# Four-layer convolution network on one core: the routing's first linear layer has its weights loaded during the attention, into columns of the last four blocks of x; those blocks are sent later, and unread products fill PE's gaps

## The reference

```python
p = x.reshape(b, c, 16, h // 16, 16, w // 16).mean(axis=(3, 5))
r = relu(einsum('bcij,oc->boij', p, conv_w) + conv_b)      # 16 channels x 256 positions
r = relu(r.reshape(b, -1) @ fc_w.T + fc_b)                 # 4096 -> 256, "first linear layer" below
rw = sigmoid(r.reshape(b, 4, c))
cw = einsum('beo,eoikl->boikl', rw, w_experts)             # 3x3 kernels of a convolution in 16 groups
out = grouped_conv(x, cw)
```

## Time and profile before

| | |
|---|---|
| median of 3 runs | 2512.54 us (2510.32 to 2512.96) |
| profiled execution | 2514.1 us, span 2512.3 us, mean granted clock 0.936 |
| PE | busy 2145.5 us (85%), 7223 records |
| DVE | 1876.6 us (75%) |
| ACT | 1435.7 us (57%) |
| POOL | 1426.0 us (57%) |
| chain that ended last | PE 48%, issue 12%, ACT 11%, DVE 10%, POOL 10%, DMA 6% |
| DMA | 172.76 MB, mean 69 GB/s |

### The profile page before, as it was taken

The page is one execution under the profiler, slowest core; times in us unless marked ns, Lnnn a source line. Parts: engine busy times, 40 slices in busy tenths (PEclk is TensorE's granted clock), DMA queues, the critical chain, the costliest instruction groups (busy, mean ns, idle before and its releaser), DMA issues.

```text
span 2512.3 us, 28673 instructions
## 1 busy us (share of the span) xinstructions
PE 2145.5 (85%) x7223; PEld 1124.5 (45%) x7223; DVE 1876.6 (75%) x3247; ACT 1435.7 (57%) x2268; POOL 1426.0 (57%) x1287
## 2 busy tenths in 40 slices
PE   2898869897968999997988977698989599999798
PEld 2397535443543333333335964353345333333343
DVE  6556766599957999985865668566999489999755
ACT  1843544386865767663346446236778467777532
POOL 2332009498947888872322400485989388888532
PEclk9988989999989999997997998799999799999899
DMA  5000283500001112224720006533000011212344
GB/s 184 1 1 1 87 296 94 190 1 1 1 1 26 40 41 56 42 51 142 238 44 1 1 1 222 191 101 152 1 1 1 11 26 38 59 38 48 88 118 118
DMA packets 199337, 172.76 MB, mean 69 GB/s; under 512 B 72535, under 2 KB 175327, under 8 KB 195831
## 3 DMA queue, kind: packets, MB, share of 16 engines
q1 hardware_dynamic: 199159, 170.78, 23.5%
HBM read 81.69 MB, written 72.29 MB: 61 GB/s over the span
## 4 chain that ended last, share of the span: by engine, by line
PE 48%; issue 12%; ACT 11%; DVE 10%; POOL 10%; DMA 6%; SPq 1%; DVEq 0%; ACTq 0%; POOLq 0%
PE PSUM L2264 8%; PE PSUM L731 6%; PE PSUM L2085 5%; DMA BIG<-BIG 4%; PE PSUM L1053 3%; POOL BIG L932 3%; PE PSUM L2128 3%; PE PSUM L2142 2%; PE PSUM L2284 2%; DVE PSUM L1117 2%; PE PSUM L1045 2%; POOL BIG L1765 2%; POOL BIG L1762 2%; PE PSUM L2100 2%; PE PSUM L2133 1%
## 5 line engine op out<-in xcount | busy, mean ns | idle before, releaser
L848 DVE TENSOR_TENSOR BIG<-PSUM,BIG 128x512 f32<-128x512 f32 x576 | 390.7, 684 | 92.4 <-PE PSUM L1045 48.0
L932 POOL TENSOR_TENSOR BIG<-BIG 128x512 f32<-128x512 f32 x320 | 407.0, 1272 | 63.6 <-ACT BIG L1019 28.6
L1117 DVE SCALAR_TENSOR_TENSOR PSUM<-BIG,VECS,PSUM 128x1024 f32<-128x1024 f32 x224 | 288.2, 1287 | 38.3 <-PE PSUM L2085 33.2
L772 POOL TENSOR_TENSOR BIG<-TOEP,BIG 128x384 f32<-128x384 f32 x84 | 98.2, 1195 | 317.6 <-DVEq L1542 317.6
L1045 PE MATMUL PSUM<-BIG,SELB 120*128 120x512 bf16 x576 | 211.7, 386 | 64.6 <-DMA BIG<-BIG 58.3
L1053 PE MATMUL PSUM<-BIG,CSTS 128*128 128x512 f32 x512 | 266.2, 601 | 0.0
L2085 PE MATMUL PSUM<-BIG,WDW 128*128 128x512 f32 x512 | 234.3, 602 | 12.4 <-ACT BIG L1989 12.4
L2264 PE MATMUL PSUM<-BIG 128*128 128x381 f32 (+1 forms) x576 | 189.1, 492 | 12.9 <-DVE BIG L779 12.9
L1045 PEld LDWEIGHTS PSUM<-BIG,SELB 120*128 120x128 bf16 x576 | 50.8, 97 | 305.4 <-DVE BIG L848 149.3
L2085 PEld LDWEIGHTS PSUM<-BIG,WDW 128*128 128x128 f32 x512 | 97.5, 193 | 140.3 <-issue 115.7
L1762 POOL TENSOR_TENSOR BIG<-BIG 128x1024 f32<-128x1024 f32 x64 | 151.1, 2360 | 10.3 <-POOL BIG L1765 10.3
(11 more groups left out here) (360 smaller groups left out, 5159.9 us busy)
## 6 DMA issues: line engine op xcount, KB each, us to landing
spill<-X SPq DMA_DIRECT2D x18, 1024.0 KB, 6.4
back_spill<-BIG SPq DMA_DIRECT2D x32, 576.0 KB, 3.4
X<-x SPq DMA_DIRECT2D x32, 512.0 KB, 7.4
rows_spill<-X SPq DMA_DIRECT2D x64, 256.0 KB, 4.2
out<-BIG SPq DMA_DIRECT2D x64, 256.0 KB, 3.6
BIG<-rows_spill SPq DMA_DIRECT2D x28, 512.0 KB, 5.2
X<-back_spill SPq DMA_DIRECT2D x14, 896.0 KB, 11.5
BIG<-fc SPq DMA_DIRECT2D x8, 1024.0 KB, 9.7
```

The lines of the kernel that those rows point to most:

```text
L772: eng.tensor_tensor(to.rearrange("p (x c r) -> p x c r", x=3, r=WROW), TOEP[:, y].unsqueeze(1).unsqueeze(1).broadcast_to([P, 3, WCH, WROW] ...
L848: dve.tensor_tensor(img(product_buffer(b, q)), img(PSUM[:, (k + q) % 2, :]), pch(c, XBASE, dy, dx), ALU.mult).then_inc(df_p, 1)
L932: pool.tensor_tensor(a, a, x, ALU.add).then_inc(df_add, 1)
L1117: return dve.scalar_tensor_tensor(out=rows8(to), in0=strip(c, base, dy, dx), scalar=vc(weights, j), in1=rows8(acc), op0=ALU.mult, op1=ALU.add)
```

## The change

The weights' tile FCT moves from WTAIL into WN: for unit o of WN, columns 640 to 1151, which are the blocks 5 to 8 (`FC_FROM` = 9 - 2*256/128 = 5). RB stays where it was. The sync queue issues the four `fc` transfers ahead of the window loop, after a wait for the first `mha_pe` of the pair. In the window loop all nine spills stay where they were in order, but only blocks 0 to 4 are read back there. Behind the loop come the wait for all squares, RT, then a wait for the second `rt_pe` (the end of L2233), then blocks 5 to 8. PE gets products of 128x512 with the constant matrix "mean" into PSUM bank 2, which nobody reads: four after the attention's output stage, one after the group norm, three after L2233, four after L2239.

```diff
+WARM = (4, 1, 3, 4)
...
+FC_FROM = WINDOWS - 2 * FC // W
...
-        FCT = r.take(RED, 2, FC)
+        FCT = WN[:, :, FC_FROM * W:WINDOWS * W].rearrange("p u (h f) -> p u h f", h=2)
+        r.at += RED * 2 * FC
...
                 def spread(w):
 
-                    sp.wait_ge(moved[w % 2], pair * MOVES[w % 2] + (w // 2 + 1) * 16)
+                    sp.wait_ge(moved[w % 2], pair * MOVES[w % 2] + (SPREAD[w % 2] if w >= FC_FROM else (w // 2 + 1) * 16))
...
+                sp.wait_ge(mha_pe, pair * 3 + 1)
+                settle(sp)
+                for j in range(4):
+                    sp.dma_start(FCT[:, 4 * j:4 * j + 4], fc[:, 4 * j:4 * j + 4]).then_inc(fc_in[j // 2], 16)
                 for w in range(WINDOWS):
                     sp.wait_ge(o_x, pair * NS + (window_strip(w) + 1 + CREDIT))
-                    if w == WINDOWS - 1:
-                        sp.wait_ge(l1_sq, (pair + 1) * (2 * NS) + CREDIT)
-                        for j in range(4):
-                            sp.dma_start(FCT[:, 4 * j:4 * j + 4], fc[:, 4 * j:4 * j + 4]).then_inc(fc_in[j // 2], 16)
-                        sp.dma_start(RT, rt_spill).then_inc(rt_in, 16)
                     sp.dma_start(spill[w], X[:, STEP * w:STEP * w + WROW, :].rearrange("p r x -> p (r x)")).then_inc(moved[w % 2], 16)
-                    if w >= 1:
+                    if 1 <= w <= FC_FROM:
                         spread(w - 1)
-                spread(WINDOWS - 1)
+                sp.wait_ge(l1_sq, (pair + 1) * (2 * NS) + CREDIT)
+                settle(sp)
+                sp.dma_start(RT, rt_spill).then_inc(rt_in, 16)
+                sp.wait_ge(rt_pe, pair * 3 + 2)
+                settle(sp)
+                for w in range(FC_FROM, WINDOWS):
+                    spread(w)
...
+                def warm(n):
+
+                    for _ in range(n):
+                        pe.matmul(PSUM[:, 2, :], cs("mean"), CSTS[:, 0:CH], start=True, stop=True)
+
                 in_turn(pe, NS // 2, 0, 1, step)
 
+                warm(WARM[0])
                 group_norm(pair * 4 + 1)
+                warm(WARM[1])
                 pe.wait_ge(l1_mom, pair * 16 + 5)
...
                 ins.then_inc(rt_pe, 1)
+                warm(WARM[2])
                 pe.wait_ge(rt_dve, pair * 16 + 16)
...
                 ins.then_inc(rt_pe, 1)
+                warm(WARM[3])
```

## The result

| | before | after |
|---|---|---|
| median of 5 runs each | 2512.54 us (2510.32 to 2515.6) | 2522.57 us (2519.57 to 2526.82) |
| ratio to before, 95% interval | | 1.0041 (1.0026 to 1.0056) |
| profiled execution | 2514.1 us, span 2512.3 | 2519.57 us, span 2517.8 |
| PE records | 7223 | 7271 (the fillers' 24 per pair) |

The forecast was 2512.9 us with 2507 to 2520 around it. The kernel became 10.0 us slower, clear of the 5.0 us that count as a difference.

What follows compares the result with a forecast made beforehand. The grouped convolution's start was taken to bound the kernel, with ACT's late blocks setting it after the change. Pair 0 at +0.9 and pair 1 at -0.5 us summed to +0.4: 2512.9 us from 2512.54, range 2507 to 2520.

Steps and rivals of the forecast that it cites:

- What bounds the kernel: Routing of each pair: the grouped convolution's start moves the end by as much; ACT's input is close behind as second limit.
- Part 1: Attention: fc transfers moved there cost nothing; the first linear layer starts at 346.2 and 1577.75, not 350.31 and 1582.48.
- Part 2: First linear layer: fillers give full clock, it takes 7.06 us and ends 6.0 and 7.4 us earlier.
- Rival A: First linear layer: clock falls as now, it starts at half clock; 4.1 us more, 2517.0 us; chance 0.20.
- Part 3: Four late blocks of x after the layer: 16.7 us to ACT; convolution starts +0.9 and -0.5 us against before.
- Rival B: Late blocks: four queued move faster, at 379 GB/s, 2.77 us each; 2508.9 us; chance 0.17.
- Rival C: Late blocks: four move no faster than one alone, 4.64 us each; +7.7, 2520.2 us; chance 0.10.
- D: First linear layer: weights not earlier or something else awaited, convolution 7.0 and 6.9 us later; 2526.4 us; chance 0.02.
- Part 4: Remaining fillers and edits around the routing: cost nothing; the last filler gives nothing, the convolution starts at half clock.
- The sum: Whole kernel: +0.9 - 0.5 = +0.4 us over both pairs, giving 2512.9 us as the median.

## Why the prediction was wrong

**What bounds the kernel: right.** The start of the grouped convolution is what moves the end, up to what the later stages scatter, and ACT's input took over from DVE's as the late one, in both pairs.

**Part 1, the fc transfers: right.** L2248 waits for DVE (0.63 us) and not for a transfer; four issues stand at 224 us. The layer starts 5.4 us behind the group norm in pair 0, as computed (346.2 - 340.8), and 4.9 us in pair 1, where the clock fell later. The group norm itself began 1.2 us later than before (341.95 against 340.78); in the nine other kernels with the early transfers it began between 340.6 and 342.8, and in the two with the transfers of before at 340.7 and 341.9, so no loss in the attention is shown.

**Part 2, the layer at full clock: wrong; this is the step that failed.** 7.06 us were put down, 9.57 and 9.62 measured: 2.5 + 2.5 us. The argument was one row with a gap of 4.06 us over which the clock stood. With a gap of 1.94 us left, 3.6 us of fillers ahead of it and one product behind the group norm, the clock fell before the layer in both pairs of all five kernels that have these fillers and the early weights, and the layer took 9.4 to 9.8 us. It fell in the gap's wake in some and only behind the next filler in others. With 0.22 us and two products it stood in both pairs of three kernels (7.08 us each time). One gap survived is no proof for a shorter one, and the row itself warned of it: the clock that stood from 359.3 to 363.4 fell soon after, with nothing on PE but the eight small records of L2239:

```profile
364.00:366.00 2.00, 0.01 (x2) 0.00 (x0) 1.91 (x2) 0.00 (x0) 0.00 (x0) 0.62 1.06 321
```

The last filler says the same. With the same gap of 1.28 or 1.29 us ahead of L2255 it took 5.40 us, partly at half clock, in both pairs of the changed kernel and in pair 0 of its repetition, and 3.70 at full clock in pair 1 of that. What fixes the moment of the fall stays open. Rival A had the mechanism, but at 1.94 us a pair and a chance of 0.20.

**Part 3, the late blocks: right in mechanism, a term too small.** 16.7 us were put down, 18.18 and 17.96 measured: 1.5 + 1.3 us. The larger part of it is the fetch of instructions, 1.0 us, which no part of the prediction had. The rest is the rate: in a full queue of nothing but these blocks (362 to 372)

```profile
DMA packets 1466, 2.90 MB, mean 290 GB/s; under 512 B 48, under 2 KB 48, under 8 KB 1466
```

it is 290 GB/s, 3.62 us a block, and not 305.5. Without the fetch it took 16.8 to 17.2, close to the 16.7. Rival B, that many transfers in flight go at 379 GB/s or more, falls, and with it the estimate from the Trainium skill (DMA: Bandwidth & Descriptors, "Bandwidth", 425 GB/s for large amounts, there issued from GpSimd): this case's rate is 290 for runs of 512 bytes. Rival C (4.64 us a block) falls too. D did not happen.

**Part 4, fillers at no cost: half right.** They delay nothing by their own length that matters, the one at half clock (2.05 us) less than 0.1 us. That the last filler gives nothing is confirmed where ACT comes late, as is the half-clock start; with the blocks split, fillers in that place do shorten the convolution (92.6 us with seven products, 94.7 and 94.8 without fillers). That adding instructions moves an instruction fetch into a queue that the path waits for was missed.

**The sum.** 5.0 us from the clock and 2.8 from the blocks make 7.8, close to the 7.7 us between +0.4 and +8.1 (the layer's earlier start in pair 1, 0.5 us, and the 0.28 us from its end to the first issue, where 0.05 was put down, cancel); the rest of the measured +10.0 is within what the later stages scatter. The range ended at 2520 because I treated the clock and the blocks as alternatives; both occurred, and together they are past it (2512.9 + 5.0 + 2.8 = 2520.7).

## What to carry to other kernels

When data is moved out of a wait by borrowing another transfer's place, the borrowed transfer's whole time goes behind the new release; split it so that only what the next engine needs first is on the path (here 8 us per pair for the same bytes). Unread products are worth nothing until they fill enough: with 1.94 us left of the gap ahead of the group norm they gave nothing, with 0.22 us left and a second product behind it 2.5 us per layer; no run lies between. Price independent misfortunes together, not as rivals: a range built from one at a time is too short on that side.

## What was unexpected of the hardware

A 16 KB instruction fetch among the late blocks is one packet of 1.2 us (0.4% of what 16 DMA engines have in 18.1 us, so one engine's time), and the landing of the transfers spread over all of them is 1.1 us later with it in the mean of the table (18.06 against 17.00), whether it comes near the end (15.7 us behind the first issue) or in the middle (8.5 us). The clock fell at 342.1 in pair 0, just behind an idle gap of 1.94 us, stood over the same gap in pair 1, and stood over one of 4.06 us in the routing of the kernel before. And the same stage took 147.8 to 152.6 us with nothing but the granted clock to tell the executions apart.
